# Self-attention of a decoder layer on one core: heads in row and column strips of TensorE, one row of sums per head, inverses spread by selector matmuls

## The reference

```python
x = x + cross_attention(layernorm(x), ctx)         # 2048 keys a batch, 16 heads of 32
# self-attention, 16 heads of DH = 32, 128 tokens a batch, clamp to [1e-7, 1 - 1e-7]
q = clamp((h @ Wq.T + bq) * scaling); k = clamp(h @ Wk.T + bk); v = clamp(h @ Wv.T + bv)
w = clamp(einsum('bhtd,bhsd->bhts', q, k))
o = clamp(einsum('bhts,bhsd->bhtd', clamp(softmax(w)), v))
x = x + clamp(o @ Wo.T + bo)
x = x + expert_choice_ffn(layernorm(x))            # 8 experts, 512 -> 2048 -> 512, 32 tokens a batch each
```

## Time and profile before

| | |
|---|---|
| Median of 3 runs | 516.55 us (515.41 to 517.08) |
| Profiled execution, its own time | 516.39 us |
| Its span | 514.6 us, so 1.8 us lie around it |
| PE busy | 455.7 us, 89% of the span |
| DVE, ACT, POOL busy | 380.9, 294.2, 89.8 us |
| Cross-attention and its output | up to about 200 us |
| Projections of the self-attention | about 200 to 228.5 us |
| Self-attention, output, gate logits | 228.5 to 288.4 us |
| Router | 288.4 to 306.2 us |
| Experts | from 306.2 us |

### The profile page before, as it was taken

The page is one execution under the profiler, slowest core; times in us unless marked ns, Lnnn a source line. Parts: engine busy times, 40 slices in busy tenths (PEclk is TensorE's granted clock), DMA queues, the critical chain, the costliest instruction groups (busy, mean ns, idle before and its releaser), DMA issues.

```text
span 514.6 us, 9233 instructions
## 1 busy us (share of the span) xinstructions
PE 455.7 (89%) x3118; PEld 379.9 (74%) x3118; DVE 380.9 (74%) x502; ACT 294.2 (57%) x605; POOL 89.8 (17%) x82
## 2 busy tenths in 40 slices
PE   0998999999993788999997279999999999999993
PEld 0877888888882667889886278878787777878782
DVE  4688677766777677458675566989898989898963
ACT  0355656666663312476422138778778787787842
POOL 4000000000006011010000802231414050504000
PEclk9998999999998699999998579999999999999997
DMA  7970000000100560200040094999999999999102
GB/s 217 337 271 21 23 22 21 21 21 21 37 4 0 198 252 1 82 1 0 2 164 1 1 326 155 341 327 348 315 357 323 358 315 363 314 359 305 65 0 82
DMA packets 42907, 81.94 MB, mean 159 GB/s; under 512 B 2952, under 2 KB 3080, under 8 KB 42888
## 3 DMA queue, kind: packets, MB, share of 16 engines
q1 hardware_dynamic: 39576, 76.16, 42.6%
q10 hardware_dynamic: 3312, 5.52, 3.1%
HBM read 80.58 MB, written 1.10 MB: 159 GB/s over the span
## 4 chain that ended last, share of the span: by engine, by line
PE 67%; DVE 13%; ACT 9%; issue 5%; DMA 2%; ACTq 2%; SPq 1%; DVEq 1%; POOL 0%; POOLq 0%
PE po L1347 17%; PE pk L1347 9%; PE pv L1347 9%; PE pv L1053 5%; ACT big_a L415 5%; PE ps L1117 4%; PE ps L1069 3%; DVE mc L741 3%; PE pv L1069 3%; PE po L1366 3%; PE ps L1110 2%; DMA att_w<-in_wq 2%; PE pk L1069 2%; PE ps L1238 2%; PE ps L1387 1%
## 5 line engine op out<-in xcount | busy, mean ns | idle before, releaser
L998 DVE TENSOR_TENSOR w_lo<-att_w,w_hi 128x2048 fp32r<-128x2048 f32 x60 | 137.8, 2306 | 24.9 <-ACT w_hi L571 24.9
L571 ACT CAST w_hi<-att_w 128x2048 fp32r<-128x2048 f32 x60 | 115.0, 1917 | 15.4 <-PE po L1347 15.4
L415 ACT ACTIVATE big_a<-ps,negm 128x128 f32<-128x128 f32 x176 | 62.2, 403 | 31.9 <-DVE negm L744 31.9
L1347 PE MATMUL po<-w_hi,ht_hi 128*128 128x512 f32 x128 | 51.9, 405 | 0.0
L1347 PE MATMUL po<-w_hi,ht_lo 128*128 128x512 f32 x128 | 50.6, 395 | 0.0
L1347 PE MATMUL po<-w_lo,ht_hi 128*128 128x512 f32 x128 | 50.5, 395 | 0.0
L1043 PE MATMUL pk<-ctx_s,att_w 128*128 128x128 f32 x352 | 45.2, 290 | 0.6 <-DMA ctx_s<-in_ctx_t 0.6
L1043 PEld LDWEIGHTS pk<-ctx_s,att_w 128*128 128x128 f32 x352 | 43.1, 203 | 3.0 <-issue 2.0
L415 ACT ACTIVATION_READ_ACCUMULATOR big_a<-ps,negm 128x1 f32 x176 | 42.8, 243 | 0.0
L741 DVE TENSOR_REDUCE mc<-ps 128x8 f32<-128x1024 f32 x22 | 26.8, 1220 | 13.7 <-PE ps L1110 13.7
L1347 PEld LDWEIGHTS po<-w_hi,ht_lo 128*128 128x128 f32 x128 | 24.1, 188 | 5.7
(11 more groups left out here) (266 smaller groups left out, 1023.4 us busy)
## 6 DMA issues: line engine op xcount, KB each, us to landing
att_w<-in_w SPq DMA_DIRECT2D x64, 1024.0 KB, 6.0
ctx_s<-in_ctx_t SPq DMA_DIRECT2D x11, 256.0 KB, 2.6
x_s<-in_x SPq DMA_DIRECT2D x1, 1024.0 KB, 5.6
att_w<-in_wk SPq DMA_DIRECT2D x1, 1024.0 KB, 7.9
att_w<-in_wq SPq DMA_DIRECT2D x1, 1024.0 KB, 10.5
att_w<-in_wv SPq DMA_DIRECT2D x1, 1024.0 KB, 7.1
att_w<-in_wo ACTq DMA_DIRECT2D x1, 1024.0 KB, 6.5
att_w<-in_sq ACTq DMA_DIRECT2D x1, 1024.0 KB, 9.9
```

The costliest lines, as they stand in the source:

```text
L415: ins = a.activation(big_a[:, h], ps[:, c, g * P:(g + 1) * P], ACT.Exp, bias=negm[:, h:h + 1], accum_out=sums[:, h:h + 1])
L571: a.copy(w_hi[:, i % SLOTS], att_w[:, i]).then_inc(hi_ok, 1)
L998: v.tensor_tensor(w_lo[:, i % SLOTS], att_w[:, i], w_hi[:, i % SLOTS], ALU.subtract).then_inc(lo_ok, 1)
L1347: ins = mm(dst, l, r, start=start and i == 0, stop=i == len(terms) - 1, skip_group_check=True)
```

## The change

- **Scores** (`scores2(b)`): a head's product contracts over its own 32 partitions only, in one of four row strips; 16 matmuls for a whole batch into the four banks of `ps`. `q_wide`, `widen` and the clearing by POOL go.
- **Exponentials and clamp**: `exps2(b, half)` (ACT) reads the scores from PSUM, and `clamp_probs(b, half)` (DVE) clamps the exponentials in SBUF, in place, between exp(LO) and exp(HI). `big_a` and `big_b` now hold a batch each.
- **Values and sums** (`values2(b)`): each head is a column strip; values come out with the head's dimensions on partitions, which is the layout that the output projection wants. The sums are 16 more column-strip matmuls with a stationary of ones and zeros (`of_group`) that gathers them as one row per head in `po[:, 1, 0:128]`.
- **Inverse** (`inverse_sums`, `spread_inverse`): one reciprocal of 128x128, then four 128x128 matmuls with a selector (`spread`) copy each head's inverse over its 32 rows; `values_copy` (ACT) brings the values to SBUF, and `normalise` multiplies and clamps.
- `turn_out` and its evacuation go: `attended_hi` (ACT) and `attended_lo` (DVE) split the result in two parts straight from `norm`.
- **Around it**: the lo part of tile 1 moves on DVE behind the last `normed_batch`; tile 3 goes from POOL to ACT (behind the last output projection) and DVE (behind the router's last PSUM reads), and so SP's wait ahead of expert 1's loads ends there. The logits go to `ps`, `weighted` gets memory of its own, and POOL's `norm_lo` waits for `normed[4]` of all batches.

The diff (semaphore declarations, and most of what is removed, are left out; the functions of before stand above):

```diff
+EXP_LO, EXP_HI = math.exp(LO), math.exp(HI)
...
-        q_wide = att_w[:, 6:8].rearrange("p i c (g t) -> p i c g t", g=KC)
...
-        weighted = big_a[:].rearrange("p h k -> p (h k)")[:, 0:B * E * CAP].rearrange("p (e b s) -> p e b s", b=B, e=E)
+        weighted = weighted_s[:].rearrange("p (e b s) -> p e b s", b=B, e=E)
+        spread = q_now
+        of_group = ctx_s[:, 3].rearrange("p (g m) -> p g m", g=KC)
+        row_sums = kt_s[:, 3]
...
-        logits = po[:, 1, 8 * HV:8 * HV + B * E]
+        logits = ps[:, 0, 0:B * E]
...
-                    sp.wait_ge(s2_mm, 2 * B)
+                    sp.wait_ge(att_lo_ok, 7)
...
-            for i in range(2):
-                pool.wait_ge(att_lo_ok, 5 + 2 * i)
-                g.memset(att_w[:, 6 + i], 0.0).then_inc(cleared, 1)
+            for i in range(KC):
+                g.tensor_copy(spread[:, i].rearrange("p (j d) -> p j d", d=DH),
+                              ident[:].rearrange("p (j d) -> p j d", d=DH)[:, :, i:i + 1].broadcast_to([P, STRIPS, DH])).then_inc(spread_ok, 1)
+            pool.wait_ge(spread_ok, KC)
+            g.memset(of_group, 0.0).then_inc(spread_ok, 1)
+            pool.wait_ge(spread_ok, KC + 1)
+            for i in range(KC):
+                g.memset(of_group[:, i].rearrange("p (m i) -> p m i", i=KC)[:, :, i:i + 1], 1.0).then_inc(spread_ok, 1)
             inverse_roots(2)
             pool.wait_ge(o2_mm, B)
+            pool.wait_ge(normed[4], B)
             for b in range(B):
                 pool.wait_ge(norm_hi_ok, b + 1)
                 if b:
                     pool.wait_ge(norm_lo_ok, b)
                 g.tensor_tensor(norm_lo[:, b], norm[:, b], norm_hi[:, b], ALU.subtract).then_inc(norm_lo_ok, 1)
-            pool.wait_ge(norm_lo_ok, B)
...
-            def widen(b):
...
-            def exps2(u):
...
+            def exps2(b, half):
+                act.wait_ge(s2_mm, b + 1)
+                if b >= 2:
+                    act.wait_ge(pv2_mm, b - 1)
+                a.activation(probs2(b, half), ps[:, 2 * half:2 * half + 2].rearrange("p c n -> p (c n)"), ACT.Exp).then_inc(e2_ok, 1)
+            def values_copy(b):
+                act.wait_ge(pv2_mm, b + 1)
+                a.copy(norm[:, b], po[:, 0]).then_inc(ot2_out, 1)
+            def attended_hi(b):
+                act.wait_ge(ot_ok, b + 1)
+                a.copy(of_batch(tr_hi, b), norm[:, b].rearrange("p (k t) -> p k t", k=KC)).then_inc(tr_hi_ok[3], 1)
             def gate_transposed(b):
                 act.wait_ge(tr_mm[4], b + 1)
                 a.copy(tr_gate[:, b], turned(4, b)).then_inc(tr_hi_ok[4], 1)
-            exps2(0)
-            exps2(1)
-            widen(2)
+            for b in range(2):
+                for half in range(2):
+                    exps2(b, half)
+            values_copy(0)
             split_first(1, v2_mm)
-            for u in range(2 * B):
...
+            attended_hi(0)
+            exps2(2, 0)
+            exps2(2, 1)
+            values_copy(1)
+            attended_hi(1)
+            exps2(3, 0)
+            exps2(3, 1)
+            values_copy(2)
+            attended_hi(2)
+            gate_transposed(0)
+            values_copy(3)
+            attended_hi(3)
+            gate_transposed(1)
+            split_first(3, o2_mm)
...
-            def clamp_scores(u):
...
+            def clamp_probs(b, half):
+                dve.wait_ge(e2_ok, 2 * b + half + 1)
+                v.tensor_scalar(probs2(b, half), probs2(b, half), EXP_LO, EXP_HI, ALU.max, ALU.min).then_inc(p2_ok, 1)
+            def inverse_sums(b):
+                dve.wait_ge(pv2_mm, b + 1)
+                if b:
+                    dve.wait_ge(inv_mm, b)
+                v.reciprocal(row_sums, po[:, 1, 0:P]).then_inc(inv_ok, 1)
+            def normalise(b):
+                dve.wait_ge(inv_mm, b + 1)
+                dve.wait_ge(ot2_out, b + 1)
+                v.tensor_tensor(norm[:, b], norm[:, b], po[:, 1], ALU.mult).then_inc(pv2_out, 1)
+                dve.wait_ge(pv2_out, b + 1)
+                v.tensor_scalar(norm[:, b], norm[:, b], LO, HI, ALU.max, ALU.min).then_inc(ot_ok, 1)
+            def attended_lo(b):
+                dve.wait_ge(tr_hi_ok[3], b + 1)
+                v.tensor_tensor(of_batch(tr_lo, b), norm[:, b].rearrange("p (k t) -> p k t", k=KC),
+                                of_batch(tr_hi, b), ALU.subtract).then_inc(tr_lo_ok[3], 1)
...
-            clamp_scores(0)
-            clamp_scores(1)
+            clamp_probs(0, 0)
+            clamp_probs(0, 1)
             split_first(1, 0)
-            for u in range(2 * B):
...
+            inverse_sums(0)
+            clamp_probs(1, 0)
+            clamp_probs(1, 1)
+            normalise(0)
+            inverse_sums(1)
+            attended_lo(0)
+            clamp_probs(2, 0)
+            normalise(1)
+            clamp_probs(2, 1)
+            attended_lo(1)
+            self_bias(0)
+            inverse_sums(2)
+            self_residual(0)
+            normalise(2)
+            clamp_probs(3, 0)
+            clamp_probs(3, 1)
+            attended_lo(2)
+            normed_batch(4, 0)
+            self_bias(1)
+            inverse_sums(3)
+            self_residual(1)
+            normalise(3)
+            normed_batch(4, 1)
+            attended_lo(3)
+            self_bias(2)
+            self_residual(2)
             normed_batch(4, 2)
             self_bias(3)
             self_residual(3)
             normed_batch(4, 3)
+            split_first(2, 1)
...
+            split_first(3, 3)
...
-            def waits_scores2(u):
-                pe.wait_ge(wide_ok, 4 * (u // 2 + 1))
-                if u == 0:
+            def scores2(b):
+                if b == 0:
                     pe.wait_ge(q2_out, KC)
                     pe.wait_ge(k2_out, KC)
-                if u >= 2:
...
+                if b:
+                    pe.wait_ge(e2_ok, 2 * b)
+                for g in range(KC):
+                    for c in range(STRIPS):
+                        r = slice(c * DH, (c + 1) * DH)
+                        ins = mm(ps[:, c, g * P:(g + 1) * P], kt2[r, b, g], qt[r, b, g], start=True, stop=True, skip_group_check=True)
+                ins.then_inc(s2_mm, 1)
+            def values2(b):
+                if b == 0:
                     pe.wait_ge(v2_out, B)
-                if u >= 2:
...
+                    pe.wait_ge(spread_ok, 1 + 2 * KC)
+                else:
+                    pe.wait_ge(pv2_out, b)
+                pe.wait_ge(p2_ok, 2 * b + 2)
+                half = big_a if b % 2 == 0 else big_b
+                for g in range(KC):
+                    for c in range(STRIPS):
+                        mm(po[c * DH:(c + 1) * DH, 0, g * P:(g + 1) * P], v_s[:, b, c * KC + g, 0:DH], half[:, c * KC + g],
+                           start=True, stop=True, skip_group_check=True)
+                    for c in range(STRIPS):
+                        ins = mm(po[c * DH:(c + 1) * DH, 1, 0:P], of_group[:, g], half[:, c * KC + g],
+                                 start=g == 0, stop=g == KC - 1, skip_group_check=True)
                 ins.then_inc(pv2_mm, 1)
+            def spread_inverse(b):
+                pe.wait_ge(inv_ok, b + 1)
+                for g in range(KC):
+                    ins = mm(po[:, 1, g * P:(g + 1) * P], spread[:, g], row_sums, start=True, stop=True, skip_group_check=True)
+                ins.then_inc(inv_mm, 1)
...
-            for u in range(2):
...
+            scores2(0)
+            scores2(1)
+            values2(0)
+            spread_inverse(0)
+            scores2(2)
+            values2(1)
+            spread_inverse(1)
+            out_project(0)
+            scores2(3)
+            values2(2)
+            spread_inverse(2)
+            out_project(1)
+            values2(3)
+            turn_gate(0)
+            spread_inverse(3)
+            out_project(2)
+            gate_project(0)
+            turn_gate(1)
             out_project(3)
+            gate_project(1)
             turn_gate(2)
-            gate_project(2, 2 * B)
+            gate_project(2)
             turn_gate(3)
-            gate_project(3, 2 * B)
+            gate_project(3)
...
-                pe.wait_ge(lo_ok, SLOTS if isinstance(e, int) and e == 0 else e * 8 + (q + 1))
+                pe.wait_ge(lo_ok, (2, 3, 3, 4)[q] if isinstance(e, int) and e == 0 else e * 8 + (q + 1))
```

More of the change, by code:

```diff
@@ L1 @@
+import math
 from contextlib import ExitStack
@@ L214, in of_batch, with probs2 @@
             return tensor[:, :, b * T:(b + 1) * T]
+        def probs2(b, half):
+            p = big_a if b % 2 == 0 else big_b
+            return p[:, 8 * half:8 * half + 8].rearrange("p h k -> p (h k)")
         def chunk_j(eng, t):
@@ L1235, in score2 @@
-            def score2(u, n):
-                b, g, c = u // 2, n // 2, 2 * (u % 2) + n % 2
-                return mm(ps[:, c, g * P:(g + 1) * P], kt2[:, b, g], q_wide[:, b % 2, c, g], start=True, stop=True)
-            def value2(u, n):
```

(17 more changed lines are left out.)

120 lines of the change are left out of this document (6 added, 114 removed).

## The result

The changed kernel took 499.16 us, the median of 4 runs (497.47 to 499.95), beside 515.98 us for the kernel before: a ratio of 0.9657, 95% interval 0.9622 to 0.9693. The forecast was 499.1. The profiled execution took 499.95 us with a span of 498.2, where 516.39 and 514.6 stood before: 16.4 us less.

What follows compares the result with a forecast made beforehand. TensorE was taken to bound the self-attention. Start 227.4, work 28.8, waits 5.0, tail 8.25 and clock 2.4 gave 271.9 against 288.4 us; this 16.5 plus the router's 0.75 gave 17.3 off 516.4: 499.1 us, range 495 to 506.

Steps and rivals of the forecast that it cites:

- TensorE is the bound and its work the gain: Self-attention: TensorE sets the pace; its work per batch falls by 3.8 us, leaving 28.8 us through the fourth output projection.
- Drain at a change of form: Rival: TensorE empties at each of 15 changes between strips and full array, 0.15 us each; 501.4 us, chance 0.08.
- The wait for the exponentials: Second batch's scores wait for both exponentials of the first, leaving TensorE idle 2.3 us; later batches hide this.
- The 1.1 us for the fourth values and two handovers: TensorE waits ahead of the fourth values, for clamps queued behind a residual, and at two handovers: 1.1 us.
- The wait for the inverse: Each spread waits for a 0.3 us reciprocal plus 0.2 drain, three times; 1.6 us with handovers.
- VectorE only just fits: VectorE's work in the stage is about 30 of 34 us; rival that VectorE or ScalarE bounds: 507 us, chance 0.07.
- Clock: One TensorE stretch at 1.2 GHz, 1.6 us, plus half another, 0.8; rival of three or more further: 504 to 512, chance 0.08.
- The prediction's stretch during the fourth projection: The low-clock stretch that slowed the old kernel's fourth output projection was kept in the forecast, 1.6 us.
- Start of the stage: POOL's memset gives way to smaller work, gaining 1.1 of TensorE's 1.34 us idle; first scores at 227.4 us.
- End: Last projection ends at 261.2 us before 2.4 for the clock; the tail to the router's first reduction takes 8.25.
- Router: VectorE's L971 falls from 1.03 to 0.3 us once POOL's L375 no longer runs beside it; 0.75 us gained.
- Experts: Expert 1's weights, requested 15 us later, cost nothing: 1.7 us in hand at worst, 8.1 at the median.

Runs made afterwards that it cites:

- e2: The changed kernel with each score matmul contracting over all 128 partitions instead of a head's row strip; 507.3 us.
- e3: The changed kernel with the reciprocal covering only 32 of its 128 columns; ratio 0.9567 to the kernel before.
- e4: The changed kernel without rows of sums and spread: ones put each head's sums on its 32 rows, reciprocal of 512 columns; 512.9 us.
- e6: The changed kernel reordered: next scores (last batch: third projection) between a batch's values and its spread of inverses; ratio 0.965 to the kernel before.
- e7: The changed kernel with both the last value projection cut in two around the first scores and the other order; ratio 0.9632 to the kernel before.
- e8: The changed kernel with SyncE waiting for all eight split tiles of expert 0 before requesting expert 1's weights; 506.3 us.
- e10: The changed kernel with tile 3's hi part behind the router's copies and POOL's norm_lo two before, two behind the router's multiply; ratio 0.9663 to the kernel before.
- e11: The changed kernel in its own order with only the first three spreads moved to PSUM bank pk; ratio 0.9656 to the kernel before.
- e1: The kernel before with only the edits beside the attention: norm_lo later, tile 3 split by ACT and DVE, tile 1's lo part later; ratio 0.9956.
- e5: The changed kernel with the last value projection cut in two, six matmuls before and six behind the first scores; ratio 0.9603 to the kernel before.
- e9: Cut projection and new order, plus three spreads in bank pk, tile 3's hi part later, norm_lo split around the router's multiply; 493.2 us.

## Why the prediction was right, point by point

- **TensorE is the bound and its work the gain.** Right: e2 puts the work of the scores back and the time comes back with it. Scores 1.10 us instead of 1.0, values and sums 1.96 instead of 2.0, a spread 0.91 instead of 0.9.
- **Drain at a change of form** was a rival at 0.15 us each. A price is there, but small. Scores in row strips begin 1.09 us behind the start of a spread, full-array scores 0.99 (e2, 239.58 to 240.57), which leaves 0.10 us for the step from full array to row strips; and 16 row strips behind the full array take 1.10 us, where those of the earlier trace rows, which stand behind other row strips, take 1.01. That is some 0.2 us an entry, estimated at 0.6 us for the three entries that are clear of a wait. The step from row to column strips lies in the 1.10 and the 1.01 alike, so these rows do not price it. The Trainium skill has a change of tiling mode drain TensorE (TensorEngine Tiling, Tiling Modes); the rows agree with a cost at the change and do not show what makes it.
- **The wait for the exponentials:** 2.3 forecast, 2.06 found, and clamps behind it hidden as said. Right. The 1.1 us for the fourth values and two handovers hardly came: TensorE is idle 5.9 us in "proj.", 2.06 + 3.73 of it for exponentials and inverses.
- **The wait for the inverse was the mis-sized term.** I took 0.3 us for 128 columns "at a column a cycle like the other VectorE rows". It is 0.96, and 3.36 for 512, so (3.36 - 0.96)/384 = 6.3 ns a column; my nearest row, 8 columns in 0.21 us, could not tell a base from a slope, and as an upper bound it would have allowed far more. TensorE stood 3.7 us for the four inverses, where I had 1.6; e3 confirms it with 2.4 us back for 0.6 us an instruction.
- **The sum was right in part by luck.** Waits in "proj." are 5.9 us in place of 5.0. The work is some 30.1 (31.7 busy less 1.6 for the low clock) in place of 28.8, in small pieces: projections of 2.9 to 3.1 us in place of 2.85, scores of 1.10, transpositions of 0.66. Against these 2.2 us stand 0.8 of the 2.4 for the clock, which came with 1.6, and the tail's 0.15. At the router's first reduction the forecast was still 1.25 us early (271.9 against 273.15); the experts were 0.4 shorter. The profiled execution is 0.85 above the forecast and happens to be 0.8 above the runs' median, so the agreement of 499.1 with 499.16 says little; that the time lies within 1 us of the sum is what the parts support.
- **VectorE only just fits.** Right, and close: e4 put 2.4 us more a batch on it and "proj." lost 14. In e6 and e7, too, TensorE waits for VectorE's results first.
- **Clock.** Half a chance for one stretch behind the first idle time, 0.8 us. It came in the change, in its repetition, in e3, e8 and e10, and not in e2, e4, e6 and e11, with the same 2.0 to 2.1 us of idleness in all nine, and it costs 1.6 (37.6 against 36.0). The prediction's stretch during the fourth projection did not come: 248 to 265 us have 1.00. That one stretch came in place of the other is luck for the sum.
- **Start of the stage:** 227.4 forecast, 227.45 and 227.03 found. The norm took 0.55 us in place of 2.00 beside POOL's small copies, and TensorE's 1.34 us are gone with the memset. The scatter of 1 us between kernels that are alike up to there is as large as this term.
- **End:** 265.1 us for the last projection against 261.2 + 2.4 = 263.6, for the reciprocals above all and the work; tail 8.1 against 8.25.
- **Router:** 0.75 forecast, 0.74 found (17.05 to 16.3), but not by the way named. L981's operation gave 0.8; L972's took 0.2 more than before; the rest, 0.15, is the gather, which took 5.9 us in place of 6.0. That the total agrees is luck. e1 had 2.0, with a multiply of 0.27, because POOL's pieces happened to lie otherwise there (last section).
- **Experts:** no DMA among the waits; with the request at 295.5 us and the first use at 309.1, 13.6 us were there for a landing of 6.8 in the middle, so 6.8 in hand where 8.1 were forecast: right. e8 shows that 12.4 us more use it up.

## What to carry to other kernels

Look a reciprocal's price up for its number of columns before it is put between two steps of the bound engine: put it on as few columns as the layout allows, and put another step of that engine beside it. A reorder that hides one wait can uncover the next one on the same buffer, so read which semaphore the following step waits for, and free that (here: another PSUM bank) in the same edit: TensorE was idle 5.9 us with the bank alone, 6.3 with the order alone, 4.7 with the fill alone, 4.9 with order and fill, and 3.4 with order, fill and bank. Judge edits of this size by the parts of a timeline, since a low stretch of TensorE's clock that comes in one profile and not in the next is as large as they are. And see that a part holds the same work on both sides: e6 looks 1.1 us faster in "proj." because 1.5 us of work had moved behind its end.

## What the runs showed of the hardware that was not expected

**A small VectorE multiply of two SBUF tensors waits for the end of POOL's running instruction.** In the change, the view of POOL's line of `norm_lo` (durations in ns, minimum, median and maximum), and windows within its second piece and at the end of its third (columns as in the earlier trace rows, POOL is the fifth pair):

```profile
L383 POOL TENSOR_TENSOR tr_lo<-norm,tr_hi x4: 1260/1262/3192, 269.5 to 275.6; 128x512 fp32r<-128x512 f32 x4
```

```profile
273.38:273.57 0.19, 0.00 (x0) 0.00 (x0) 0.19 (x1) 0.00 (x0) 0.19 (x1) 0.50 0.00 0
275.45:275.60 0.15, 0.04 (x1) 0.04 (x1) 0.06 (x1) 0.00 (x0) 0.01 (x1) 0.50 0.00 0
```

POOL is busy 0.01 us of the second window, so its piece ends at 275.46 us (the fourth starts at 275.6), and VectorE's multiply of 128x32, begun at 274.30, at 275.51. In e10 POOL had nothing to do at that moment, and the same multiply took 0.19. In the records of the 13 other profiles the multiply lasts 0.27 to 1.22 us and ends 0.045 to 0.048 us behind the end of the POOL instruction that was running, in every one: its length is what was left of that instruction. In the first window, a VectorE subtraction of the same size that takes one input from PSUM kept its 0.19 us while POOL was busy throughout. The other way round, POOL's first piece took 3.19 us beside VectorE's 2.29 us split, where it takes 1.26 alone. The Trainium skill (SBUF — State Buffer, SBUF: two separate sides) has POOL and a VectorE instruction with two SBUF inputs share an exclusive lock that is held for a whole instruction; the traces agree. VectorE's rows behind the multiply, a copy from PSUM and the searches for maxima, kept their 0.28 us beside POOL.

**The same idle time does or does not bring TensorE to 1.2 GHz.** Nine profiles with 2.0 to 2.1 us of idleness at the same place: five fell, four did not. With 0.46 to 0.48 us there (e5, e7, e9) none of three fell, which is too few to say that the shorter idle time prevents it.
